# First layer of a hybrid kernel: the output projection's second half in two parts, the triangles over four row groups around V's second half, and the inverse begun behind two corrections

## The reference

```python
q = silu(x @ Wq.T); k = silu(x @ Wk.T); v = x @ Wv.T      # 16 heads of 32
beta = 2.0 * sigmoid(x @ Wbeta.T)
k = k * rsqrt(sum(k * k) + EPS)                            # per head
# per token, per head: delta = beta * (v - k @ S); S += outer(k, delta); o = q @ S
gate = sigmoid(x @ Wg1.T @ Wg2.T)
og = o * gate;  og = og * rsqrt(mean(og * og) + EPS) * g_norm
x = x + og @ Wo.T
```

## Time and profile before

| | us |
|---|---|
| three runs | 4949.72 to 4962.0 |
| median | 4955.77 |
| the profiled execution | 4960.62 |
| its span, first to last instruction | 4958.5 |
| PE busy in the span | 4588.3 (93%) |
| DVE busy | 3635.6 (73%) |
| ACT busy | 2411.9 (49%) |
| POOL busy | 720.6 (15%) |
| from the first step's chain to the 31st step's, 30 steps | 127.9 to 1933.9 |

### The profile page before, as it was taken

How to read it: one execution, slowest core, us unless ns; L and a number is a source line. 1 busy time by engine, 2 the same in 40 slices (tenths; PEclk the granted TensorE clock), 3 DMA queues, 4 the chain that set the end, 5 groups by cost and what they waited for, 6 DMA issues and landing times.

```text
span 4958.5 us, 144788 instructions
## 1 busy us (share of the span) xinstructions
PE 4588.3 (93%) x63104; PEld 3209.3 (65%) x63104; DVE 3635.6 (73%) x7890; ACT 2411.9 (49%) x4592; POOL 720.6 (15%) x909
## 2 busy tenths in 40 slices
PE   7999999999999998699999999999999999999998
PEld 7787777777787776555655654664664665565564
DVE  6677777766676665578778778778778877877876
ACT  3333343333343332366466456457456546546645
POOL 0000000000000000121221221221221122122121
PEclk8999999999999998899999999999999999999999
DMA  2222222222222221100000000000000000000000
GB/s 85 55 63 72 64 69 65 67 67 66 65 63 63 63 63 49 62 2 18 18 1 19 18 2 18 18 2 18 18 18 2 18 18 2 18 18 2 18 10 10
DMA packets 352134, 171.76 MB, mean 35 GB/s; under 512 B 300016, under 2 KB 300784, under 8 KB 350736
## 3 DMA queue, kind: packets, MB, share of 16 engines
q1 hardware_dynamic: 342528, 145.20, 10.9%
q10 hardware_dynamic: 8976, 17.30, 1.2%
HBM read 93.74 MB, written 67.63 MB: 33 GB/s over the span
## 4 chain that ended last, share of the span: by engine, by line
PE 43%; DVE 11%; ACT 2%; issue 1%; POOL 1%; DMA 1%; SPq 0%; DVEq 0%; ACTq 0%; POOLq 0%
PE row_psum L1738 9%; PE row_psum L1713 9%; PE row_psum L40 5%; DVE smax L2000 5%; PE row_psum L42 5%; PE row_psum L41 5%; PE row_psum L1726 4%; PE row_psum L1786 1%; DVE xr_lo L1861 1%; PE row_psum L1766 1%; DVE probs L1980 1%; PE row_psum L1500 1%; DVE stats L1827 1%; POOL rstd L1297 1%; DMA q_stack<-shift 1%
## 5 line engine op out<-in xcount | busy, mean ns | idle before, releaser
L2000 DVE TENSOR_REDUCE smax<-row_psum 128x1 f32<-128x512 f32 x2048 | 1270.5, 685 | 91.7 <-PE row_psum L1713 88.6
L1434 ACT ACTIVATE probs<-row_psum 128x512 f32<-128x512 f32 x2048 | 1091.8, 603 | 352.2 <-PE row_psum L1726 332.9
L1713 PE MATMUL row_psum<-k_stack,q_stack 64*128 64x512 f32 (+1 forms) x2048 | 738.1, 437 | 50.8 <-DVE smax L2000 24.5
L1726 PE MATMUL row_psum<-q_stack,k_stack 64*128 64x512 f32 (+1 forms) x2048 | 733.3, 458 | 22.6 <-ACT probs L1434 8.1
L1713 PEld LDWEIGHTS row_psum<-k_stack,q_stack 64*128 64x128 f32 (+1 forms) x2048 | 350.8, 186 | 503.8 <-DVE smax L2000 372.9
L1738 PE MATMUL row_psum<-probs,v_aug 128*32 128x512 f32 x4096 | 538.9, 603 | 1.6 <-ACT av_sb L1450 0.4
L1726 PEld LDWEIGHTS row_psum<-q_stack,k_stack 64*128 64x128 f32 (+1 forms) x2048 | 319.3, 184 | 225.8 <-ACT probs L1434 155.7
L889 DVE TENSOR_TENSOR lane_t<-lane_t,lane_p 128x30 f32<-128x30 f32 (+14 forms) x960 | 318.5, 332 | 32.9
L40 PE MATMUL row_psum<-wf_hi,xr_hi 128*128 128x320 f32 (+1 forms) x1024 | 331.9, 324 | 4.7 <-DVE xr_lo L1861 3.2
L886 DVE TENSOR_TENSOR lane_p<-lane_t 128x30 f32<-128x30 f32 (+14 forms) x960 | 316.4, 330 | 23.5
L42 PE MATMUL row_psum<-wf_hi,xr_lo 128*128 128x320 f32 (+1 forms) x1024 | 319.0, 312 | 0.0
(11 more groups left out here) (215 smaller groups left out, 9999.8 us busy)
## 6 DMA issues: line engine op xcount, KB each, us to landing
x_sp<-in_x ACTq DMA_DIRECT2D x33, 512.0 KB, 4.2
tri_dram<-tri SPq DMA_DIRECT2D x256, 64.0 KB, 2.0
lane_t<-tri_dram SPq DMA_DIRECT2D x32, 512.0 KB, 4.6
inv_dram<-lane_t SPq DMA_DIRECT2D x32, 512.0 KB, 2.7
inv_b<-inv_dram SPq DMA_DIRECT2D x256, 64.0 KB, 2.3
x_res<-in_x SPq DMA_DIRECT2D x32, 512.0 KB, 3.8
x<-x_res SPq DMA_DIRECT2D x32, 512.0 KB, 3.9
xs<-x SPq DMA_DIRECT2D x16, 1024.0 KB, 5.5
```

The lines of the kernel that those rows point to most:

```text
L1434: act.activation(probs[:, h % PROBS, tt, :], ps[:, m % STACK_BANKS, :], ACT.Exp, scale=float(DH) ** -0.5).then_inc(exp_ready, 1)
L1713: pe.matmul(ps[:, bank, :], q_stack[rows, qt, P * st:P * st + P], k_stack[rows, kv, :], start=True, stop=True).then_inc(max_mm, 1)
L1726: pe.matmul(ps[:, m % STACK_BANKS, :], k_stack[rows, kv, P * tt:P * tt + P], q_stack[rows, qt, :], start=True, stop=True).then_inc(score_m ...
L2000: dve.tensor_reduce(smax[:, g, st:st + 1], ps[:, bank_of("max", NT * g + st), :], AX.X, ALU.max).then_inc(max_ready, 1)
```

## The change

Four edits, all in the first layer. (1) The triangles' matmuls of one t run over the pieces g, the halves and then the four row groups e, and no longer over e first; those of t = 1 wait at once for all four masked copies of t = 0. V's second half (`project_v` 1) moves between t = 0 and t = 1, and on DVE `normalise` moves between the masked copies of t = 0 and of t = 1. (2) The output projection of t = 1 is done in two parts of six matmuls, one ahead of `state_inputs` and one behind it. (3) On DVE the inverse's first piece ("split", which waits for the lanes) comes behind the first two `correct_lower` and no longer ahead of them. (4) Two columns of the inverse go from ahead of the first `advance` to behind the last one, and the second `add_residual` goes behind the first `advance`.

```diff
             def triangles(b, s, t):
-                for e in range(HPT):
-                    if t:
-                        pe.wait_ge(tri_ready, at(b, s, TS * HPT, e + 1))
-                    rows = slice(HD * e, HD * e + HD)
-                    for g in range(KT):
-                        for half in range(2):
-                            i0 = P * t + C * half
+                if t:
+                    pe.wait_ge(tri_ready, at(b, s, TS * HPT, HPT))
+                for g in range(KT):
+                    for half in range(2):
+                        i0 = P * t + C * half
+                        for e in range(HPT):
+                            rows = slice(HD * e, HD * e + HD)
                             last = pe.matmul(bank[4 + e][C * half:C * half + C, 2 * C * g:2 * C * g + 2 * C],
                                              kq[rows, g, 0, i0:i0 + C], kq[rows, g, 0:s + 2:s + 1, i0:i0 + C],
                                              start=True, stop=True)
-                    last.then_inc(kk_ready, 1)
+                            if g == KT - 1 and half == 1:
+                                last.then_inc(kk_ready, 1)
...
                 if behind:
-                    output(*behind, 1, further, ahead)
+                    output(*behind, 1, further, ahead, range(KT // 2))
                 state_inputs(*now)
+                if behind:
+                    output(*behind, 1, further, ahead, range(KT // 2, KT))
                 chain(*now, 0)
...
                     triangles(*further, 0)
+                    project_v(*further, 1)
                     triangles(*further, 1)
-                    project_v(*further, 1)
...
-                           inputs=range(23, 26), chain0=range(26, 27), chain1=range(27, 28), chain2=range(28, 29),
-                           values=range(29, NB - 1))
+                           inputs=range(23, 24), chain0=range(24, 25), chain1=range(25, 26), chain2=range(26, 27),
+                           values=range(27, NB - 1))
...
-                invert_ahead("split")
                 correct_lower(*now, 0, behind)
                 correct_lower(*now, 1, behind)
+                invert_ahead("split")
                 invert_ahead("product")
...
                 invert_ahead("transitions")
+                invert_ahead("inputs")
+                advance(*now, 0)
                 if behind:
                     add_residual(*behind, 1)
-                invert_ahead("inputs")
-                advance(*now, 0)
                 invert_ahead("chain0")
...
                 output(*now)
                 if further:
-                    triangles(*further)
+                    triangles(*further, 0)
                     normalise(*beyond)
+                    triangles(*further, 1)
```

More of the change, by code:

```diff
@@ L720, in output_sums, with output @@
                               start=True, stop=True).then_inc(ms_ready, 1)
-            def output(b, s, t, further, ahead):
-                if further:
+            def output(b, s, t, further, ahead, inputs=range(KT)):
+                if further and inputs[0] == 0:
                     if t == 0:
@@ L733, in output @@
                         pe.wait_ge(v_ready, at(*ahead, TS, TS))
-                pe.wait_ge(ohi_ready, at(b, s, TS, t + 1))
-                pe.wait_ge(olo_ready, at(b, s, TS, t + 1))
-                for k in range(KT):
+                if inputs[0] == 0:
+                    pe.wait_ge(ohi_ready, at(b, s, TS, t + 1))
+                    pe.wait_ge(olo_ready, at(b, s, TS, t + 1))
+                for k in inputs:
                     last = split3(pe, (BD, BB)[t][:, :], o_hi[:, k, P * t:P * t + P], o_lo[:, k, P * t:P * t + P],
                                   w_hi[:, 3, k, :], w_lo[:, 3, k, :], k == 0, k == KT - 1)
-                last.then_inc(wo_mm, 1)
+                if inputs[-1] == KT - 1:
+                    last.then_inc(wo_mm, 1)
             def begin(first, second, third):
@@ L896, in invert, with triangles @@
                                     lane_b[:, :]).then_inc(inv_ready, 1)
-            def triangles(b, s):
+            def triangles(b, s, t):
                 m = masks[:, :].rearrange("p (o i) -> p o i", o=1).to_broadcast([P, KT, 2 * C])
-                for t in range(TS):
-                    for e in range(HPT):
-                        dve.wait_ge(kk_ready, at(b, s, TS * HPT, t * HPT + e + 1))
-                        dve.tensor_tensor(tri[:, s, t, :, e, :], bank[4 + e][:, :].rearrange("p (g i) -> p g i", g=KT), m,
-                                          ALU.mult).then_inc(tri_ready, 1)
+                for e in range(HPT):
+                    dve.wait_ge(kk_ready, at(b, s, TS * HPT, t * HPT + e + 1))
+                    dve.tensor_tensor(tri[:, s, t, :, e, :], bank[4 + e][:, :].rearrange("p (g i) -> p g i", g=KT), m,
+                                      ALU.mult).then_inc(tri_ready, 1)
             def correct_lower(b, s, q, behind):
@@ L968, in begin @@
                 normalise(*second)
-                triangles(*first)
+                triangles(*first, 0)
+                triangles(*first, 1)
                 split_x(*second)
@@ L973, in begin @@
                 normalise_k(*second)
-                triangles(*second)
+                triangles(*second, 0)
+                triangles(*second, 1)
                 normalise(*third)
```

## The result

The changed kernel takes 4826.88 us (median of four runs, 4826.17 to 4828.11), against 4952.75 for the kernel before (four runs, 4949.37 to 4962.0). The ratio is 0.9743, with a 95% interval of 0.9726 to 0.976: 126 us or 2.6% faster. The profiled execution took 4826.68, its span is 4824.6. The forecast was 4857.

What follows compares the result with a forecast made beforehand. PE was taken as the bound, busy 95% of the steps. Terms summed to -3.25 us a step, -98 over 30 steps and about -1 for `begin`, giving 4857 us; whole range 4808 to 4912, the forecast's own 4830 to 4885.

Steps and rivals of the forecast that it cites:

- The triangles and the step's end: First triangle to `project_k`: 1.1 us a t, `project_k` at 8.45 instead of 11.45, 3.0 us a step gained.
- The sum: All terms a step: -3.0 + 0.2 - 0.45 - 0.5 + 0.4 + 0.1 = -3.25 us, over 30 steps -98.
- Rival A: Triangles' places on PE overlap less, 1.6 to 2.5 us a t: 4890 to 4935 us; chance 0.12.
- `normalise`: On DVE, now ahead of POOL's start: an estimated 1.1 us for the two, where today's take 1.98.
- The clock in V's second half: PE's half-clock spells there go because triangles shrink to 1.1 us between dense pieces: -0.45 us a step, bounds 0 and -0.45.
- The projection in two parts: Output projection on PE: a second entry and exit costs +0.2 us a step.
- The chain: Idle for "issue" and half clock in the chain, a third of it gone: -0.5 us a step, bounds 0 and -1.8.
- rival B: The chain's stalls and half-clock spells go too, -1.8 instead of -0.5: about 4818 us; chance 0.11.
- The lanes: They land later, so corrections reach PE late and it waits at `solve_fourth`: +0.4 us a step, range 0 to 1.2.
- Rival C: Slower: triangles' return slips 6 us or more, delaying the inverse and `solve_first`: 4975 us; chance 0.03.
- inv_b: Inverse's last part, issued later on DVE, lands at 5.9 us against `solve_first` at 6.2: +0.1 us a step.
- rival D: The 3 us are hidden by PE waiting at `solve_first` for the inverse: within 15 us of 4956; chance 0.03.

Runs made afterwards that it cites:

- e1: The changed kernel with the triangles' matmuls run over the row groups first again, all else as changed: 4898.97 us, ratio 0.9882.
- e8: The kernel before with only the new order of the triangles' matmuls, V's second half still behind t = 1: 4988.78 us, ratio 1.0076.
- e4: The changed kernel with the output projection of t = 1 in one piece again, ahead of `state_inputs`: 4857.29 us, ratio 0.9797.
- e13: The kernel before with edits 1 and 3 alone: triangles around V's second half, inverse's first piece behind two `correct_lower`: 4875.03 us, ratio 0.983.
- e9: The changed kernel with the inverse's columns and the second `add_residual` put back ahead of the first `advance`: 4858.24 us, ratio 0.982.

## Why the prediction was right, and where it was off

**The triangles and the step's end: right.** A t was to take 1.1 us and takes 1.14; `project_k` was to start at 8.45 and starts at 8.57. The sum had 3.0 + 0.45 for this stretch, 3.30 came. L569 fell from 151.0 us to 72.4, not to 65. Shown by e1, which undoes the order and loses 2.39 us a step there. One reading of the old order was loose: it doesn't send four matmuls running to one place. The loop over the halves was the inner one, so a row group's eight matmuls alternated between two places, both in bank 4 + e. The new order changes the row group and the bank with every matmul, and no run tells the two apart. Against the bank as the cause speaks L704, whose 32 recorded matmuls all write one bank, over four row groups, and pass in 0.28 us (1025.83 to 1026.11). The rule in "TensorE: Matmul & The Clock Gate" of the Trainium skill, section "Wait — 56ns, not 53.3ns?", no less than about 25 ns from one matmul's start to the next, fails here too: 64 recorded matmuls in 1.14 us are 18 ns each. Rival A, 1.6 to 2.5 us a t, is out.

**`normalise`: right.** 1.1 us forecast, 0.99 measured, once it lay ahead of L265; in e8, where it kept its old place, it takes 1.96. That agrees with "SBUF — State Buffer" of the Trainium skill, section "Who interferes with whom", by which the one of DVE and GpSimd that comes second is blocked from the port pair they share for the other's whole instruction. The runs show the two places and the two times, not the ports.

**The clock in V's second half: the size right, the reason in part.** The group L40 to L42 with `x_hi` and `x_lo` fell from 316.6 to 299.9 us, and no time between the first triangle and `project_k` is at half clock any more (1.06 us a step before). That is 0.56 a step over both halves of V, where 0.45 was taken for one. The reason given was that the triangles shrink from 5 us to 1.1 at a time. e1 has no half clock there either with 2.52 us a t, and e8, with 1.2 us a t but a wait of 2.7 between them, has 2.12 us a step. So it was V between the two t, not the shorter triangles, that took it away.

**The projection in two parts: right.** The six rows of each part take 1.60 and 1.59 us from the first to what follows, 3.19 together, where twelve took 3.01: +0.18, against +0.2.

```profile
1020.48 0.50 PE L40 MATMUL span_bank<-w_hi,o_hi 128*128 128x512 f32 x1
...
1022.08 1.07 PE L693 MATMUL span_bank<-uw,rhs 64*32 64x32 f32 x102
1023.98 0.34 PE L693 MATMUL span_bank<-uw,rhs 64*32 64x32 f32 x26 [0.83 <-issue]
1024.24 0.50 PE L40 MATMUL span_bank<-w_hi,o_hi 128*128 128x512 f32 x1
...
1025.83 0.45 PE L704 MATMUL span_bank<-state,gt 32*32 32x32 f32 x32
```

**The chain: the term that was mis-sized.** The sum took "a third", -0.5. The chain's stretch fell by 1.99, and of that 0.61 came back ahead of it beside the 0.18 just named. The net is -1.4, against -0.5: 27 us of the whole. Of the 1.99, 0.72 is idle time of PE (1.89 to 1.17 us a step): the stops by "issue" fell by 0.88 (1.48 to 0.60), other waits grew a little. Most of the rest is the clock. Half clock from the chain's start to the first triangle went from 3.88 us a step to 0.95, and its unchanged pieces are some 1.15 us a step less busy: L529 and L542 by 21.1 us in 30 steps, L704 and L710 by 14.5 us in 32 (against L703 and L709 in the earlier trace rows). Here it went rival B's way, who had -1.8. The argument against B was that spells begin in the chain's second half, which is unchanged. That was the step that failed: the code there is unchanged, but the spells went with the stops, as e4 (37.0 us idle, 3.88 us half clock in this stretch) and the changed kernel (17.0, 0.95) show side by side. The trace before had it too: of the 16 spells that begin between the chain's start and the first triangle, 15 begin during a stop of over 0.4 us or less than 3 us after one, and such times are 28% of that stretch. In the changed kernel 6 spells begin there, 4 of them so. The 0.61 that came back is the stop at L693 (13.2 us against 1.5, 0.39 a step) and L693's own rows, 0.15 longer a step (46.9 us in 32 steps, where L692 had 42.2). The sum had no such term, since it asked only what the cut does to the burst behind it and not to the one it leaves without cover. e13, e4 and e9 show that the chain's gain needs both edits. With one alone it is 0.6 or 0.7 a step net, with both 1.67. Edit 4 stood in the sum only as a cost.

**The lanes: a cost that didn't come.** +0.4 was taken, for a wait at `solve_fourth`. It is 5.7 us in 4 of 30 steps, 0.2 a step, and the whole stretch behind `project_k` is 0.07 shorter. The lanes did land later against the first triangle, by 1.56 us on average (15.18 to 16.74), more than the 1.1 that was worked out. But the step from which the cover was read was the latest of 28: DVE started L877 there 17.4 us after the first triangle, where the mean is 15.18. The estimate was built on an extreme. Rival C is out for the same reason; the latest start after the change is 17.61.

**inv_b: as good as no cost.** The last part of the inverse lands 5.68 us after the first triangle on average, `solve_first` wants it at 6.3, and PE waits 0.8 us for it in two of 30 steps. The 2 us that DVE was said to have to spare were there, and rival D is out.

The sum again with what was measured, a step: -3.30 at the end, -1.99 in the chain, +0.79 ahead of it, -0.07 for the rest, -4.57. Its 1.32 beyond the forecast are 0.9 of the chain, 0.57 of lanes and inverse, less 0.15 at the end. The two large misses point the same way, so the forecast isn't right by errors that cancel. It is right because the largest term, the step's end, was.

**What stays open.** That the stops by "issue" are waits for instructions is read from the traces, where it holds for every one. No run changed the supply by itself, and none changed the stops without moving other work. So how much of the half clock they cause is read from the spells and from e4 beside the changed kernel, not isolated. Whether the row group or the bank makes the new order fast is open too.

## What to carry to other kernels

Order small matmuls so that neighbours use different row groups of the array and different banks, but give the wait for those banks some dense work as cover: the order alone was 0.8% slower, with cover it is the largest part of 2.6%. Once an engine gets faster, look in the queues of the others for instructions that stand behind a DMA wait that they don't need; here that was worth 114 us. And place dense work, in parts, between bursts of small matmuls, since it gives the next 256 instructions time to arrive: a stop can be paid twice, once as idle time and once as half clock behind it. When PE waits for nothing that a view names, look at the queue for instructions.

## What the runs showed of the hardware

- 64 recorded f32 matmuls of 32 rows x 64 columns with 128 moving columns take 1.14 us (18 ns each) when the row group and the bank change with every matmul and the eight places are visited in turn. They take 2.52 us when eight matmuls running share a row group and a bank and alternate between two places.
- PE stops for up to 2.6 us in bursts of 64x32 and 32x32 matmuls at 8 to 18 ns each. All 761 such stops in 14 traces fall at one place of every 256 recorded instructions and end 1.0 to 1.6 us after a packet of 16 KB of the queue for instructions. From the packet's start to its first instruction it is at least 2.15 us.
- With 12 dense matmuls (3 us) ahead of both bursts and none between them the stops in these lines are 42.5 us in 30 steps, with six and six 30.2, with 4, 2 and 6 21.2, with all twelve behind the first burst 61.4.
- After such a stop of 2.42 us, dense 128x512 matmuls took 0.63 us each and then 0.39 again.
- Twelve dense matmuls between bursts of small ones take 3.01 us in one piece and 1.60 + 1.59 in two, 0.18 more.
